# Autocorrelation weights transformed at plain delays, output split into an even and an odd part in time

## The reference

```python
qf = jnp.fft.fft(q, axis=2)            # q: layernorm(x), k and v: ctx
kf = jnp.fft.fft(k, axis=2)
corr = jnp.fft.ifft(qf * jnp.conj(kf), axis=2).real
topk = int(C * np.log(L))              # 11 delays of L = 256
w, idx = jax.lax.top_k(corr.transpose(0, 1, 3, 2), topk)
w = jax.nn.softmax(w, axis=-1)
for i in range(topk):
    g = jnp.minimum(idx[:, :, None, :, i] + pos, L - 1)
    out = out + w[:, :, None, :, i] * jnp.take_along_axis(v, g, axis=2)
```

## Time and profile before

| what | us |
|---|---|
| median of 3 runs (lowest, highest) | 2205.26 (2202.94, 2205.42) |
| profiled execution, its own time | 2206.25 |
| profiled execution, its span | 2204.5 |
| PE busy | 2055.3 (93%) |
| DVE busy | 1115.2 (51%) |
| ACT busy | 1166.5 (53%) |
| POOL busy | 627.2 (28%) |

### The profile page before, as it was taken

The page is one execution under the profiler, slowest core; times in us unless marked ns, Lnnn a source line. Parts: engine busy times, 40 slices in busy tenths (PEclk is TensorE's granted clock), DMA queues, the critical chain, the costliest instruction groups (busy, mean ns, idle before and its releaser), DMA issues. The chain is left out here.

```text
span 2204.5 us, 25816 instructions
## 1 busy us (share of the span) xinstructions
PE 2055.3 (93%) x9634; PEld 1027.0 (47%) x9634; DVE 1115.2 (51%) x1951; ACT 1166.5 (53%) x1827; POOL 627.2 (28%) x624
## 2 busy tenths in 40 slices
PE   7882999999999999999999999999857799999997
PEld 6771444444444444444444444444333455555543
DVE  6884243252524334252423425252546888888862
ACT  5666665656566565656656565655223344444420
POOL 1111221212121121212111121211234666677641
PEclk9995999999999999999999999999967899999999
DMA  5533211111111111111111121111111011111000
GB/s 193 172 120 97 69 48 54 48 50 61 49 54 48 57 52 50 54 50 53 55 55 48 49 58 53 54 48 39 70 45 57 15 39 48 48 49 43 15 30 29
DMA packets 58493, 128.37 MB, mean 58 GB/s; under 512 B 8704, under 2 KB 9344, under 8 KB 58368
## 3 DMA queue, kind: packets, MB, share of 16 engines
q1 hardware_dynamic: 58368, 126.72, 18.1%
HBM read 118.30 MB, written 8.39 MB: 57 GB/s over the span
## 5 line engine op out<-in xcount | busy, mean ns | idle before, releaser
L615 ACT ACTIVATE level<-level 128x512 f32<-128x512 f32 x924 | 581.7, 630 | 29.4
L809 PE MATMUL ps_ring<-xT_hi,gu_hi 128*128 128x512 f16 x1376 | 522.4, 380 | 2.8 <-DVE rel L736 2.8
L809 PE MATMUL ps_ring<-xT_hi,gu_lo 128*128 128x512 f16 x1376 | 522.1, 379 | 0.0
L809 PE MATMUL ps_ring<-xT_lo,gu_hi 128*128 128x512 f16 x1376 | 522.1, 379 | 0.0
L725 DVE SCALAR_TENSOR_TENSOR wt<-level,w_scale,absm 128x512 f32<-128x512 f32 x132 | 98.9, 749 | 496.9 <-ACT level L615 496.8
L744 DVE SCALAR_TENSOR_TENSOR X<-ps_ring,ffn_gain,X 128x512 f32<-128x512 f32 x352 | 260.3, 749 | 138.0 <-PE ps_ring L832 138.0
L679 POOL TENSOR_TENSOR gu_lo<-wt,gu_hi 128x512 f16<-128x512 f32 x88 | 102.8, 1168 | 767.0 <-ACT gu_hi L621 767.0
L832 PE MATMUL ps_ring<-dn_hi,hid_hi 128*128 128x512 f16 x704 | 266.9, 379 | 0.0
L832 PE MATMUL ps_ring<-dn_hi,hid_lo 128*128 128x512 f16 x704 | 266.8, 379 | 0.0
L832 PE MATMUL ps_ring<-dn_lo,hid_hi 128*128 128x512 f16 x672 | 254.6, 379 | 0.0
L809 PEld LDWEIGHTS ps_ring<-xT_hi,gu_lo 128*128 128x128 f16 x1376 | 134.6, 98 | 163.1 <-issue 1.0
(11 more groups left out here) (210 smaller groups left out, 2818.0 us busy)
## 6 DMA issues: line engine op xcount, KB each, us to landing
codes<-in_codes SPq DMA_DIRECT2D x132, 256.0 KB, 2.8
absm<-in_absmax SPq DMA_DIRECT2D x264, 128.0 KB, 3.1
X<-in_x SPq DMA_DIRECT2D x16, 512.0 KB, 4.2
c_in<-in_ctx SPq DMA_DIRECT2D x16, 512.0 KB, 5.2
cT<-in_ctxT SPq DMA_DIRECT2D x16, 512.0 KB, 3.4
xT_hi<-in_ctx SPq DMA_DIRECT2D x8, 1024.0 KB, 7.1
out<-X SPq DMA_DIRECT2D x16, 512.0 KB, 2.9
xT_hi<-in_ctx SPq DMA_DIRECT2D x16, 256.0 KB, 3.3
```

What stands on the lines that cost most here:

```text
L615: act.activation(level[u % 2][:], codes[u % RING][:] if k == 0 else level[u % 2][:], ACT.Prelu, bias=bias, scale=scale, alpha=alpha).then_ ...
L809: mm = pe.matmul(o[:], w[c][:, m, k, :], xx[:, k, ts], start=(q == 0), stop=(q == 3 * KD - 1))
```

## The change

The weights `cut` are no longer folded: `weight_turn` turns both halves of the 256 plain delays, and `weight_spectrum` transforms them with matrices over 256 delays (`delay_hi`, `delay_lo`), so each of the four spectra takes two halves by three fp16 products. `weight_even` and `weight_odd` have twelve matmuls each instead of six. `w_fold` and `wf` go, and ScalarE scales `cut` in place.

The delays being plain, the spectra at the output fit the folded time axis: two of them (`e_x`, `n_d`) give a part that is odd about the middle of time, two (`e_d`, `n_x`) a part that is even. So `output` has four fp32 matmuls, two into each half of psQ: first the odd part (`anti_mm`), then the even one (`out_mm`). `anti_out` (ScalarE) copies the odd part, times the gate, to `anti`; `add` (VectorE) adds the even part out of psQ to both halves of X (`sym_done`); `anti_add` (GpSimd, at the start of the next step) adds `anti` to one half and subtracts it from the other (`x_done`). `dc_fix` (GpSimd) puts the row of the zero frequency right. `q_spectrum(n)` waits for `sym_done` and `anti_done`. There are seven constants, of 1.4 MB instead of 1.0.

```diff
-                for name in ("fwd", "fwd_hi", "fwd_lo", "inv"):
+                for name in ("fwd", "fwd_hi", "fwd_lo", "inv", "back", "delay_hi", "delay_lo"):
...
-                def w_fold(n):
-                    if n:
-                        pool.wait_ge(wT_mm, n)
-                    for c in (0, 2):
-                        pool.wait_ge(w_done, CH * n + c + 2)
-                        for k, op in enumerate((ALU.add, ALU.subtract)):
-                            pool.tensor_tensor(wf[:, k, c:c + 2, :], cut[:, c:c + 2, 0:P], cut[:, c:c + 2, P:L][:, :, ::-1], op).then_inc(wf_done, 1)
+                def dc_fix(n):
+
+                    pool.wait_ge(wprod_comb, 4 * n + 1)
+                    pool.tensor_tensor(e_d[0:1, 0, :], e_d[0:1, 0, :], e_d[0:1, 1, :], ALU.subtract).then_inc(dc_done, 1)
+
+                def anti_add(n):
+                    pool.wait_ge(anti_done, n + 1)
+                    for t, op in enumerate((ALU.add, ALU.subtract)):
+                        pool.wait_ge(sym_done, 2 * n + t + 1)
+                        dst = X[:, 2 * (n // 2) + t, cols(n)]
+                        pool.tensor_tensor(dst, dst, anti[:], op).then_inc(x_done, 1)
...
                     window(win[0])
+                    if 0 < n <= N:
+                        anti_add(n - 1)
                     if n + 1 < N:
                         corr_comb(n + 1)
...
                         out_comb(n, 1)
+                        dc_fix(n)
...
-                        act.wait_ge(wf_done, 4 * n + 2 * (c // 2) + 2)
-                        act.activation(wf[:, :, c, :], wf[:, :, c, :], ACT.Copy, scale=rws[:, c:c + 1]).then_inc(wn_done, 1)
+                        act.activation(cut[:, c, :], cut[:, c, :], ACT.Copy, scale=rws[:, c:c + 1]).then_inc(wn_done, 1)
+
+                def anti_out(n):
+                    act.wait_ge(anti_mm, n + 1)
+                    if n:
+                        act.wait_ge(x_done, 2 * n)
+                    act.activation(anti[:], psQ[:, 1, :], ACT.Copy, scale=half_gate[:]).then_inc(anti_done, 1)
...
                         weights(n + 1)
+                    if n < N:
+                        anti_out(n)
                     window(win[3])
...
                     if n >= 2:
-                        pe.wait_ge(x_done, 2 * n - 2)
+                        pe.wait_ge(sym_done, 2 * n - 2)
+                        pe.wait_ge(anti_done, n - 1)
...
+                def weight_spectrum(k):
+                    for half in range(2):
+                        for q, (w, src) in enumerate(((delay_hi, wT_hi), (delay_hi, wT_lo), (delay_lo, wT_hi))):
+                            for h in range(2):
+                                mm = pe.matmul(psE[:, half, :], w[:, 2 * k + half, h, :], src[:, h, :], start=(q + h == 0), stop=(q + h == 3))
+                    mm.then_inc(ws_mm, 1)
...
                     pe.wait_ge(prod_done, min(2 * n + 4, 2 * N))
                     pe.wait_ge(wprod_row, n + 1)
-                    for k, src in enumerate((e_d, e_x, n_d, n_x)):
-                        pe.wait_ge(wprod_comb, 4 * n + k + 1)
-                        for t in range(2):
-                            mm = pe.matmul(psQ[:, t, :], inv[:, k, t * P:(t + 1) * P], src[:, 0, :], start=(k == 0), stop=(k == 3))
-                    mm.then_inc(out_mm, 1)
+                    pe.wait_ge(wprod_comb, 4 * n + 2)
+                    pe.matmul(psQ[:, 1, :], back[:, 1, :], e_x[:, 0, :], start=True, stop=False)
+                    pe.wait_ge(wprod_comb, 4 * n + 3)
+                    pe.matmul(psQ[:, 1, :], back[:, 2, :], n_d[:, 0, :], start=False, stop=True).then_inc(anti_mm, 1)
+                    pe.wait_ge(wprod_comb, 4 * n + 4)
+                    pe.matmul(psQ[:, 0, :], back[:, 3, :], n_x[:, 0, :], start=True, stop=False)
+                    pe.wait_ge(dc_done, n + 1)
+                    pe.matmul(psQ[:, 0, :], back[:, 0, :], e_d[:, 0, :], start=False, stop=True).then_inc(out_mm, 1)
...
                     if n:
-                        dve.wait_ge(wf_done, 4 * n)
+                        dve.wait_ge(wT_mm, n)
...
-                        dve.scalar_tensor_tensor(dst, psQ[:, t, :], half_gate[:], dst, ALU.mult, ALU.add).then_inc(x_done, 1)
+                        dve.scalar_tensor_tensor(dst, psQ[:, 0, :], half_gate[:], dst, ALU.mult, ALU.add).then_inc(sym_done, 1)
```

More of the change, by code:

```diff
@@ L863, in spectra @@
     fwd = np.stack([np.cos(even), even_im, np.cos(odd), -np.sin(odd)]).transpose(1, 0, 2)
-    scaled = fwd * DFT_SCALE
-    high = scaled.astype(np.float16)
+    weight = np.where(f == 0, 1.0, 2.0) / L
+    back_im = even_im * weight
+    back_im[:, :1] = np.sin(np.pi * t) / L
+    back = np.stack([np.cos(even) * weight, back_im, np.cos(odd) * 2 / L, -np.sin(odd) * 2 / L]).transpose(2, 0, 1)
     t = np.arange(L)[:, None]
@@ L868, in spectra @@
     nyquist = np.where(t % 2 == 0, 1.0, -1.0)
-    weight = np.where(f == 0, 1.0, 2.0) / L
     im_inv = -np.sin(even) * weight
     im_inv[:, :1] = (nyquist - 1.0) / L
-    inv = np.stack([np.cos(even) * weight, im_inv, np.cos(odd) * 2 / L, -np.sin(odd) * 2 / L])
-    return fwd.astype(np.float32), high, (scaled - high).astype(np.float16), inv.transpose(2, 0, 1).astype(np.float32)
+    inv = np.stack([np.cos(even) * weight, im_inv]).transpose(2, 0, 1)
+    delay_im = -np.sin(even)
+    delay_im[:, :1] = -nyquist
+    delay = np.stack([np.cos(even), delay_im, np.cos(odd), -np.sin(odd)]).reshape(4, 2, P, P).transpose(2, 0, 1, 3)
+    scaled = [fwd[:, :2] * DFT_SCALE, delay * DFT_SCALE]
+    high = [m.astype(np.float16) for m in scaled]
+    low = [(m - h).astype(np.float16) for m, h in zip(scaled, high)]
+    return {"fwd": fwd.astype(np.float32), "inv": inv.astype(np.float32), "back": back.astype(np.float32),
+            "fwd_hi": high[0], "fwd_lo": low[0], "delay_hi": high[1], "delay_lo": low[1]}
 def phase_tail(nc, io, res):
@@ L894, in sem @@
             return ctx.enter_context(nc.semaphore("a_" + name))
-        fwd, fwd_hi, fwd_lo, inv, const_in, ctx_in = (res[k] for k in ("fwd", "fwd_hi", "fwd_lo", "inv", "const_in", "ctx_in"))
+        fwd, fwd_hi, fwd_lo, inv, back, delay_hi, delay_lo = (res[k] for k in ("fwd", "fwd_hi", "fwd_lo", "inv", "back", "delay_hi", "delay_lo"))
+        const_in, ctx_in = res["const_in"], res["ctx_in"]
         c_in = [res[f"ctx_in{s}"] for s in range(2)]
@@ L1078, in _ @@
                 k_fold(2)
-                w_fold(0)
                 for n in range(N + LAG):
@@ L1281, in weight_even @@
                     pe.wait_ge(k_done, min(n + 2, N))
-                    for half in range(2):
-                        mm = dft_parts(psE, half, half, wT_hi[:, half, :], wT_lo[:, half, :])
-                    mm.then_inc(ws_mm, 1)
+                    weight_spectrum(0)
                 def weight_odd(n):
                     pe.wait_ge(wprod_done, 4 * n + 2)
-                    for half in range(2):
-                        mm = dft_parts(psE, half, 2 + half, wT_hi[:, 1 - half, :], wT_lo[:, 1 - half, :])
-                    mm.then_inc(ws_mm, 1)
+                    weight_spectrum(1)
                 def output(n):
@@ L1589, in build @@
         place, start = res["xT_hi"][:].rearrange("p k t -> p (k t)"), 0
-        for name, shape, dt in (("ctx_in0", [2, D], F32), ("ctx_in1", [2, D], F32), ("fwd", [4, P], F32), ("inv", [4, L], F32), ("last", [BANK], F32),
-                                ("fwd_hi", [4, P], HALF), ("fwd_lo", [4, P], HALF), ("wT_hi", [2, BANK], HALF), ("wT_lo", [2, BANK], HALF)):
+        for name, shape, dt in (("ctx_in0", [2, D], F32), ("ctx_in1", [2, D], F32), ("fwd", [4, P], F32), ("inv", [2, L], F32), ("back", [4, P], F32), ("last", [BANK], F32),
+                                ("fwd_hi", [2, P], HALF), ("fwd_lo", [2, P], HALF), ("delay_hi", [4, 2, P], HALF), ("delay_lo", [4, 2, P], HALF), ("wT_hi", [2, BANK], HALF)):
             size = int(np.prod(shape)) * (2 if dt is F32 else 1)
@@ L1663, in layouts @@
     bound_q = np.stack([s.reshape(P, -1) for s in (*absmax_of, np.pad(a["L0_ffn_d_absmax"], ((0, 0), (0, padf // QBLK))))], 1)
-    fwd, fwd_hi, fwd_lo, inv = spectra()
     arrays = {
@@ L1668, in layouts @@
         "w1": a["L1_ffn_W"].reshape(KD, P, D).transpose(1, 0, 2),
-        "fwd": fwd, "fwd_hi": fwd_hi, "fwd_lo": fwd_lo, "inv": inv,
+        **spectra(),
         "x": a["x"], "ctx": a["ctx_4096"],
```

14 lines of the change are left out of this document (6 added, 8 removed).

## The result

The changed kernel took 2212.51 us (median of 7 runs, 2211.46 to 2213.85); the kernel before, 2205.78 in seven runs. Ratio 1.0031, 95% interval 1.0019 to 1.0043: slower by 0.3%. The profiled execution took 2213.49 us with a span of 2211.6, 7.1 us more than before.

A forecast was written before the change was run, and what follows sets the result against it. TensorE was full at 29.82 us a step, with VectorE's loop of 28.95 just under it and expected to become the bound. +7.4 (stretch) + 2.0 (start) - 2.7 (end) = +6.7 us, giving 2212.0 us; range 2202 to 2223.

The forecast's parts named there:

- the likeliest case: VectorE's loop sets the period of the full stretch, 30.2 to 30.8 us; total 2208 to 2216 us; chance 0.5.
- full stretch: Eleven periods from `n_d` of step 3 to that of step 14: 30.5 us each against 29.82, +7.4 us.
- steps 0 to 2: Opening stage: `weights` earlier without the fold, but shorter `output` opens holes at lower clock; +2 us, bounds -2 and +5.
- the end: Steps 14 and 15: +0.7 us in step 14, -3.4 from the shorter `output` in step 15; together -2.7.
- The loop: From `weight_odd` through VectorE to `add`, then `q_spectrum` to `weight_odd` on TensorE: 28.95 us, 31.53 with the added matmuls.
- The saving on VectorE: In `select`, without GpSimd's fold beside it, the L1481 block ends at 11.35 instead of 12.36: -1.0 us a period.
- `k_fix` beside `anti_add`: GpSimd's two additions delay VectorE's `k_fix` by up to 0.5 us, covered until `weight_even` by about 0.4; booked 0.
- The tie on ScalarE: ScalarE's chain to `low` ends 16.2 us after `n_d`, TensorE reaches `linear` at 16.3; booked 0, bound +0.3.
- TensorE as the bound: Rival for the full stretch: TensorE's work still sets the step, -0.86 us a period, total 2192 us; chance 0.11.
- a fallen clock in the full stretch: Rival: holes on TensorE lower its clock, +1 to +2 us more a period, total 2225 to 2235; chance 0.07.
- The locks go altogether: Rival: VectorE's waits beside GpSimd all vanish, period 29.7 us, total 2203, no difference; chance 0.14.
- No saving: Rival: other GpSimd work replaces the fold beside VectorE, or ScalarE's tie fails; period 31.0 to 31.5, total 2217 to 2224; chance 0.18.

The follow-up runs named there:

- the last reordered run: Changed kernel with its work reordered on VectorE, ScalarE and GpSimd, plus GpSimd's `add(now,1)` moved behind the next step's `corr_comb`: 2200.44 us, ratio 0.9976 to the kernel before.

## Why the prediction was right

2212.0 was predicted, 2212.5 measured, by the likeliest case. By its steps, per period where nothing else is said:

| step | predicted | measured |
|---|---|---|
| `weight_even`, `weight_odd` | 2.58 each | 2.59, 2.60 |
| end of the L1481 block after `n_d` | 11.35 | 11.35 and 11.52 |
| end of `add` after `n_d` | 14.05 | 14.04; 14.20 in odd steps |
| `q_spectrum` to the next `n_d` | 13.80 + 2.58 = 16.38 | 16.25; 16.60 in odd steps |
| period | 30.5 | 30.39 and 30.90, mean 30.57 |
| full stretch, eleven periods | +7.4 | +8.25 |
| steps 0 to 2 | +2 | +1.05 |
| the end | -2.7 | -2.2 |

The stretch came out 0.85 us higher, the start 0.95 lower, the end 0.5 higher than booked. That the total is right within half a us is the cancelling of these, and luck; that it is a slowdown of this size is not, since the stretch makes nearly all of it.

*The loop.* It stands: padding in it is paid (4.55 of 4.7 us), padding beside it is free, shortening it by order alone gives 12 us back in the stretch (336.30 to 324.25), and the same order does nothing in the kernel before. TensorE's own sum did fall: `output` has four matmuls, and the engine is busy for 29.26 us of 30.39 in step 8 and for 29.06 of 29.42 in the last reordered run, where 28.96 had been worked out. What the prediction didn't see is the second way round, over ScalarE's `weights`, `anti_out`, `even_out` and `high(nxt,1)` to `low(nxt,1)`, `k_fix` and `weights_low`. It checked ScalarE against `linear` alone. In every second period this way is the longer one, by 0.35 us.

*The saving on VectorE.* It came as worked out: 0.98 us in even steps, 0.82 in odd ones. The last L1481 lost its 0.52. In even steps L1466 gave back (0.41 in step 8) and the first L1509 took most of it (1.09 instead of 0.88), since `k_fold` ends 9.99 us after `n_d` (10.47 in the kernel before; 10.0 to 10.5 was booked). In odd steps it is the other way: L1466 took 1.25 and every L1509 0.42. GpSimd's L1039 (1.26 us from 1945.43) ended at 1946.69, and the L1509 that started beside it at 1945.88 took 1.09 us and ended at 1946.97, where the next ones took 0.41. The Trainium skill (SBUF — State Buffer, "Who interferes with whom") says that a VectorE operation with two SBUF inputs and a GpSimd operation that reads SBUF exclude each other, the later one standing until the first is done. With that the trace agrees in the main: L1509 ended behind the GpSimd operation, though only 0.28 us behind it, less than the 0.41 it takes alone.

*`k_fix` beside `anti_add`.* This is the term that was booked wrong, at 0 with a bound of +0.5. The cover ahead of `weight_even` was thought to be about 0.4 us and wasn't enough in odd steps, where the power computation comes first. The late start of `anti_add` cost 0.36 us in every second period, 1.8 us of the stretch as the run with `rstd_of` early shows (336.30 to 334.49); the additions altogether cost 2.25, as the run without them shows (334.05). That is more than the difference between +7.4 and +8.25, because the plain loop came out at 30.39 and not 30.5.

*`dc_fix`, constants, ScalarE.* `dc_fix` takes 1.26 us and nobody waits for it. The seven constants are issued between 1559.31 and 1562.84 and nobody waits for them. The tie on ScalarE held for `linear`: `low(nxt,1)` ends at 1952.66, `linear` starts at 1953.01, as soon as TensorE gets there.

*The start.* The hole ahead of the low-rank product of the 14th unit opened as forecast, and the clock fell with it:

```profile
1727.59 3.78 PE L1339 MATMUL a_psL<-l_x,l_prod 32*128 32x512 f32 x4 [4.40 <-DVE l_E L1537]
```

0.34 us of idle time became 4.40, and 1.98 us became 3.78. The stage as a whole cost 1 us and not 2: `n_d` of step 0 comes 3.4 us earlier (1672.35 against 1675.71), that of step 2 2.3 us later (1753.25 against 1750.91), that of step 3 1.05 later. Which part of the fold's going gave that gain wasn't tried alone.

*The end.* `weight_odd` of step 15 again starts behind a hole of 2.53 us, but the clock falls in the middle of it:

```profile
2144.86 0.60 PE L1305 MATMUL a_psE<-xT_hi 128*128 128x512 f16 x2 [2.53 <-DVE e_x L1522]
...
2145.73 1.66 PE L1305 MATMUL a_psE<-xT_hi 128*128 128x512 f16 x4
2147.18 1.06 PE L1305 MATMUL a_psE<-wT_lo,xT_hi 128*128 128x512 f16 x2
```

The prediction had the first six at 1.2 GHz, as in the earlier trace rows, and the added six at 2.4: 4.0 us. Here the granted clock was 1.00 for the first five or so and 0.50 for the others: 4.23 us. The sum is near, the course another; this agreement is luck. `linear` of step 14 came 1.5 us sooner and not 1.9, so from `n_d` of step 14 to that of step 15 it took 1.3 us more and not 0.7; what follows took 3.5 less (3.4 booked). In the run without `anti_add` the same hole of 2.53 us was followed by twelve matmuls at the full clock. Whether it falls there varies between kernels that differ little, so this term is uncertain by 1.6 us.

*The rivals.* TensorE as the bound and a fallen clock in the full stretch are excluded for the changed kernel by the windows; in the two kernels with less work on TensorE (six matmuls, half an `output`) the clock did fall. "The locks go altogether" is excluded by L1509 at 1.09 and a period of 30.4. "No saving" would have been a period of 31.0 to 31.5.

## What to carry to other kernels

An engine at 100% is the bound, but a loop over several engines may lie just under it, and then the next saving meets that loop. Follow one buffer from the instruction that frees it round to the same instruction a step later, and add up; the gap to the step's length is about all that a saving on the full engine can bring, and a cost inside the loop beyond that gap is paid in full. Follow every engine's part: the loop found first need not be the only one near. Here 3.43 us taken from TensorE beside the loop and 2.58 put into it made the kernel slower, and moving a few instructions (`add` straight behind `select`, what can go before it into `select`) made the same work faster than either kernel.

## What the runs showed that was not expected

Beside the loop through `add` and `q_spectrum` lies a second one, from `select` over ScalarE to `low(nxt,1)`, `k_fix` and `weights_low`. In the changed kernel it is the longer one in every second period, by 0.35 us; in the kernel before, `weights_low` of step 9 ended at 1984.32, only 0.55 us before `weight_even` started. The waits of VectorE's operations beside GpSimd's belong to both. A move that takes one of them away can bring another (`k_fix` 1.64 to 0.69 us, `nmax` 0.41 to 0.86, and nothing gained), so a part of what is saved on one engine comes back on another.

With TensorE's work reduced by 3.43 us (kernel before, half an `output`) or by 2.58 (changed kernel, six matmuls), the periods were uneven, 27.8 to 30.8. The longest, 30.35 to 30.75, are all those with a granted clock of 0.94; the rest of the unevenness goes with `nmax`, L1509 and `k_fix` beside GpSimd. So taking work from the full engine opened holes, and in three or four of eleven periods 0.4 to 1.5 us of the saving went to the slower clock. In the changed kernel the holes are 0.5 to 0.65 us, and the clock stayed at 1.00. Why the clock fell behind some holes of 1.3 to 1.9 us before `turn` and not behind others of the same length isn't known, and no run took the GpSimd waits away alone in those two kernels.
